# Key and query products of a delta-rule scan: plain stores, scatter in the loads, eight key rows first

## The reference, cut to what matters

```python
q = silu(causal_conv4(x @ Wq.T)); k = silu(causal_conv4(x @ Wk.T)) * SCALE; v = silu(causal_conv4(x @ Wv.T))
a = sigmoid(x @ Wa.T + ba); beta = sigmoid(x @ Wb.T + bb)
def step(S, inp):                       # S: batch, head, 64 value rows, 64 key columns
    qt, kt, vt, at, bt = inp
    err = einsum('bhij,bhj->bhi', S, kt) - vt
    S = at[..., None] * S - bt[..., None, None] * (err[..., None] * kt[:, :, None, :])
    return S, einsum('bhij,bhj->bhi', S, qt)
```

## Time and profile before

| | |
|---|---|
| runs | 7149.1, 7164.11, 7169.97 us; median 7164.11 |
| profiled execution, first to last instruction (span) | 7152.7 us |
| of it, the recurrence | to about 4300 us, 64 slots of about 65 us |
| busy over the span | DVE 76%, PE 70%, POOL 51%, PE weight loads 46%, ACT 46% |
| mean granted TensorE clock | 0.799 of full |

### The profile page before, as it was taken

How to read it: one execution, slowest core, us unless ns; L and a number is a source line. 1 busy time by engine, 2 the same in 40 slices (tenths; PEclk the granted TensorE clock), 3 DMA queues, 4 the chain that set the end, 5 groups by cost and what they waited for, 6 DMA issues and landing times. The chain is left out here.

```text
span 7152.7 us, 175742 instructions
## 1 busy us (share of the span) xinstructions
PE 5027.7 (70%) x58695; PEld 3318.4 (46%) x58695; DVE 5415.6 (76%) x15973; ACT 3322.6 (46%) x7234; POOL 3637.4 (51%) x4232
## 2 busy tenths in 40 slices
PE   5666666666666766666666644888878878888878
PEld 3555555555455555555555533333444443434443
DVE  5888889888888988888888864666666666666665
ACT  4554455444445444544454422444444444444444
POOL 3778778777777877787778771111111111111110
PEclk8777778777777777877777767888888888888888
DMA  4667666766766676667667742111111111111111
GB/s 124 156 158 163 165 152 160 167 160 148 166 162 161 158 166 163 155 158 170 153 157 164 170 107 64 43 50 51 45 45 44 44 48 44 44 44 44 44 45 37
DMA packets 1186126, 804.64 MB, mean 112 GB/s; under 512 B 1038563, under 2 KB 1090435, under 8 KB 1177220
## 3 DMA queue, kind: packets, MB, share of 16 engines
q1 hardware_dynamic: 878212, 610.17, 35.3%
q10 hardware_dynamic: 307200, 185.09, 10.6%
HBM read 490.57 MB, written 304.55 MB: 111 GB/s over the span
## 5 line engine op out<-in xcount | busy, mean ns | idle before, releaser
L464 POOL TENSOR_TENSOR qp<-qp,ab 128x512 f32<-128x512 f32 (+7 forms) x1024 | 937.3, 915 | 75.3
L469 POOL TENSOR_TENSOR qp<-qp,pt 128x512 f32<-128x512 f32 (+7 forms) x1024 | 912.8, 891 | 82.2 <-issue 2.0
L1771 DVE TENSOR_REDUCE nmax<-w_bank 128x1 f32<-128x512 f32 x1024 | 642.8, 684 | 408.0 <-PE w_bank L1353 403.1
L844 DVE SCALAR_TENSOR_TENSOR p_bank<-y,conv_w,p_bank 128x128 f32<-128x128 f32 x3072 | 828.1, 349 | 74.6 <-issue 25.0
L466 POOL TENSOR_TENSOR pt<-qp,vb 128x512 f32<-128x512 f32 (+7 forms) x1024 | 813.3, 794 | 9.2 <-DVE vb L921 9.2
L1308 POOL TENSOR_TENSOR ot<-ot,ln_w 128x1024 f32<-128x1024 f32 x64 | 151.1, 2361 | 1139.9 <-ACT ot L1610 1139.9
L530 PE MATMUL d_bank<-st 64*32 64x80 f32 x16384 | 490.1, 290 | 338.4 <-issue 319.1
L1313 POOL TENSOR_TENSOR x1b<-x,bias 128x256 f32<-128x256 f32 x64 | 46.4, 725 | 1162.7 <-DVE bst L1867 1162.7
L594 PEld LDWEIGHTS p_bank<-xnT,wqkv 128*128 128x128 f32 x4096 | 547.2, 215 | 192.2 <-issue 192.2
L502 PE MATMUL d_bank<-xd,kt 32*64 32x128 f32 x7936 | 342.4, 320 | 409.8 <-DVE st L862 393.2
L594 PE MATMUL p_bank<-xnT,wqkv 128*128 128x128 f32 x4096 | 596.5, 306 | 43.0 <-ACT st L676 31.3
(11 more groups left out here) (219 smaller groups left out, 11769.4 us busy)
## 6 DMA issues: line engine op xcount, KB each, us to landing
db<-decay_dram SPq DMA_DIRECT2D x124, 1024.0 KB, 12.3
prod_dram<-prod ACTq DMA_DIRECT2D x64, 1280.0 KB, 9.7
kp<-prod_dram SPq DMA_DIRECT2D x64, 640.0 KB, 4.4
qp<-prod_dram SPq DMA_DIRECT2D x64, 640.0 KB, 6.5
a_dram<-at ACTq DMA_DIRECT2D x64, 512.0 KB
ab<-a_dram SPq DMA_DIRECT2D x64, 512.0 KB, 5.9
v_dram<-vt ACTq DMA_DIRECT2D x64, 512.0 KB
vb<-v_dram SPq DMA_DIRECT2D x64, 512.0 KB, 7.1
```

Of the source, the lines that this page charges most:

```text
L464: link(nc.gpsimd.tensor_tensor(q, q, ab[:, g, r:r + 1, :].to_broadcast([128, w, DV]), ALU.mult), 1)
L469: link(nc.gpsimd.tensor_tensor(q, q, pt2[:, 0:w], ALU.add))
L844: nc.vector.scalar_tensor_tensor(out=zz, in0=y[:, j % Y_BANKS, i, :, tap:tap + C], scalar=conv_w[:, m, tap:tap + 1], in1=zz, op0=ALU.mult, ...
L1771: nc.vector.tensor_reduce(nmax[:, n:n + 1], bank[:], AX.X, ALU.max, negate=True).then_inc(freed, 1)
```

## The change

`prod_dram` gets the layout that the products have in SBUF: [128 rows, 32 blocks, 80]. ACT stores it in two DMAs, four batches each, the first as soon as the fourth batch is copied; every partition writes one contiguous run of 5,120 bytes in each. The waits for the earlier loads from the same DRAM tensor stand ahead of the copies, not behind them. The loads now gather pieces of 320 bytes: for each head h of four, one DMA into partitions h, h+4, h+8, ... . `kp` is loaded in two sets of four DMAs, rows 0 to 7 (semaphore `kp_in`) and rows 8 to 15 (`kl_in`), and `qp` in one set of four. In SP's order the first set, with its wait for both parts of the store, stands ahead of the `upd_dram` store; the rest stays behind it. DVE's first half waits for the first set alone, POOL for the second one and for `qp`.

```diff
-    prod_dram = [dram(f"prod_dram{g}", [GB * 4, P, ROW]) for g in range(GROUPS)]
+    prod_dram = [dram(f"prod_dram{g}", [P, GB * 4, ROW]) for g in range(GROUPS)]
...
+                if valid(lo + 1, hi + 1):
+                    rows = prod_dram[o].rearrange("(h k r) m c -> h k m r c", h=4, k=2)
+                    sp.wait_ge(*dma_of(p_wr, n, g, 1, 32))
+                    held(sp, sp_passed)
+                    if valid(lo, hi):
+                        sp.wait_ge(solve_chain, SOLVE_OPS * s + FIRST_HALF_OPS)
+                        held(sp, sp_passed)
+                    for h in range(4):
+                        sp.dma_start(kp[h:128:4, 0:HALF], rows[h, 0, :, 0:HALF]).then_inc(kp_in[o], 16)
                 if updates(lo, hi):
                     sp.wait_ge(solve_chain, SOLVE_OPS * (s + 1))
...
                     sp.dma_start(upd_dram[g].rearrange("b h t i -> (b h) (t i)"), eb[:]).then_inc(upd_wr[g], 16)
                 if valid(lo + 1, hi + 1):
-                    src = prod_dram[o].rearrange("m (h k r) c -> (m h) k r c", h=4, k=2)
-                    sp.wait_ge(*dma_of(p_wr, n, g, 1))
-                    held(sp, sp_passed)
-                    if due(SOLVE_OPS * s):
+                    if valid(lo, hi):
                         sp.wait_ge(solve_chain, SOLVE_OPS * s + solved(HALF))
                         held(sp, sp_passed)
-                    elif valid(lo, hi):
-                        sp.wait_ge(solve_chain, solved(HALF))
-                        held(sp, sp_passed)
-                    sp.dma_start(kp[:], src[:, 0]).then_inc(kp_in[o], 16)
-                if valid(lo + 1, hi + 1):
+                    for h in range(4):
+                        sp.dma_start(kp[h:128:4, HALF:C], rows[h, 0, :, HALF:C]).then_inc(kl_in[o], 16)
                     if due(dma_of(o_wr, n, g, -1)[1]):
                         sp.wait_ge(*dma_of(o_wr, n, g, -1))
                         held(sp, sp_passed)
-                    sp.dma_start(qp[:, o], src[:, 1]).then_inc(qp_in[o], 16)
+                    for h in range(4):
+                        sp.dma_start(qp[h:128:4, o], rows[h, 1]).then_inc(qp_in[o], 16)
...
-                pool.wait_ge(*dma_of(kp_in, n, g, 0))
+                pool.wait_ge(*dma_of(kl_in, n, g, 0, 64))
...
-                pool.wait_ge(*dma_of(qp_in, n, g, 0))
+                pool.wait_ge(*dma_of(qp_in, n, g, 0, 64))
...
             def products(s, n, g):
                 if due(dma_of(x_wr, n, g, -1, 32)[1]):
-                    act.wait_ge(*dma_of(p_wr, n, g, -1))
+                    act.wait_ge(*dma_of(p_wr, n, g, -1, 32))
                     act.wait_ge(*dma_of(x_wr, n, g, -1, 32))
-                for b in range(GB):
-                    act.wait_ge(p_filled, 8 * s + b + 1)
-                    nc.scalar.activation(prod[:, b, :], d_bank[b % 2][:, 0:4 * ROW], ACT.Copy).then_inc(p_freed, 1)
-                act.wait_ge(p_freed, 8 * s + 8)
                 if due(dma_of(qp_in, n, g, -2)[1]):
-                    act.wait_ge(*dma_of(qp_in, n, g, -2))
-                if due(dma_of(kp_in, n, g, -2)[1]):
-                    act.wait_ge(*dma_of(kp_in, n, g, -2))
-                act.dma_start(prod_dram[g].rearrange("m p c -> p m c"), prod[:].rearrange("p b (q c) -> p (b q) c", c=ROW)).then_inc(p_wr[g], 16)
+                    act.wait_ge(*dma_of(kp_in, n, g, -2, 64))
+                    act.wait_ge(*dma_of(kl_in, n, g, -2, 64))
+                    act.wait_ge(*dma_of(qp_in, n, g, -2, 64))
+                for first in (0, GB // 2):
+                    for b in range(first, first + GB // 2):
+                        act.wait_ge(p_filled, 8 * s + b + 1)
+                        nc.scalar.activation(prod[:, b, :], d_bank[b % 2][:, 0:4 * ROW], ACT.Copy).then_inc(p_freed, 1)
+                    act.wait_ge(p_freed, 8 * s + first + GB // 2)
+                    act.dma_start(prod_dram[g][:, 4 * first:4 * first + 2 * GB].rearrange("p m c -> p (m c)"),
+                                  prod[:, first:first + GB // 2].rearrange("p b c -> p (b c)")).then_inc(p_wr[g], 16)
...
-                    dve.wait_ge(*dma_of(kp_in, n, g, 0))
+                    dve.wait_ge(*dma_of(kp_in, n, g, 0, 64))
```

## The result

The changed kernel takes 7090.91 us (median of 4 runs, 7082.73 to 7096.39) against 7156.6 (4 runs, 7135.93 to 7169.97): ratio 0.9898, 95% interval 0.9878 to 0.9918. That is just past the end of the likeliest case's own range (7095, all of the wait back), and inside the wide one (7085 to 7190). The span fell from 7152.7 to 7080.9 us, 71.8 less. The last L942 begins at 4284.3 before and its counterpart L949 at 4204.8 after, so the recurrence gave 79.5 and the untouched rest varied by 7.7 the other way.

What follows compares the result with a forecast made beforehand. Bound: the recurrence's ring through DVE, the error exchange and PE, DVE also waiting for `kp`. Removed 67.3 us, given back 10 and 5, net 52: span 7100.7, plus 11.4 to the median, 7112 us; range 7085 to 7190.

Steps and rivals of the forecast that it cites:

- likeliest case: Recurrence: DVE's wait for `kp` goes, net 52 us, 7112 us; own range 7095 to 7137; chance 0.57.
- The cap: DVE's wait for `kp` at L911, 67.3 us in 25 slots: the most an earlier `kp` can give back.
- third rival: The product store is no faster, landing at 2012.3 as before: 7179 us, 7200 if instruction fetches are held up; chance 0.07.
- More than the cap: Rival: PE's stalls move with the traffic, 7080 us; chance 0.03.
- The store: Product store in the late slot lands at 2006.8 instead of 2012.3; bounds 2003.9 and 2009.2.
- The first eight rows: Four 82 KB key loads land at 2010.8, DVE wants them at 2012.7: wait gone, 1.9 us to spare.
- Gathers at the rate of `xd`: Rival: `kp` and `qp` gather slowly, 8.0 us more in SP's queue, 7231 us; chance 0.14.
- SP's order: Twelve loads of 0.52 us, 6.2 us, replace two taking 0.8; `e_dram` goes out some 0.9 us late, mostly covered.
- first rival: SP becomes the bound: late by a mean 0.8 us, 49 us more go, 7161 us; chance 0.19.
- Given back: Off the gain: 10 us for `e_dram` beyond its cover in 25 late slots, 5 us for late store landings.
- ACT: Second DMA issue, 0.39 us, between copies of batches 3 and 4, hidden by a 0.48 us wait for PE: nothing.
- The store is no faster: Rival: product store lands at 2012.3 as before, `upd_dram` waits behind it; 7179 us at least; chance 0.07.

Runs made afterwards that it cites:

- e9: Kernel before with its product store split in two DMAs, both issued after the eighth copy, old layout and order: 7154.87 us, ratio 1.0019.
- e6: Kernel before with the order alone: key rows 0 to 7 loaded ahead of `upd_dram`, old layout, single store: 7105.91 us, ratio 0.9934.
- e8: e2 with one wait more: SP issues the two `db` loads only when `xk` has landed: 7073.27 us, ratio 0.9893.
- e4: Kernel before with its store into the old layout split in two parts, the first issued after the fourth copy: 7089.17 us, ratio 0.9905.
- e11: Kernel before with two-part store and first eight key rows ahead of `upd_dram`, old layout (edits of e4 and e6): 7083.08 us, ratio 0.9917.
- e3: Changed kernel with one 1.31 MB store after the eight copies instead of two parts: 7116.73 us, ratio 0.9939.
- e10: Changed kernel with one store after the eighth copy and all gathers behind `upd_dram` (edits of e3 and e1): 7103.69 us, ratio 0.9941.
- e7: Changed kernel with each of the four query loads cut in two, four more DMA issues on SP: 7174.90 us, ratio 1.0030.
- e1: Changed kernel with the first set of four key loads, and its wait for the store, moved behind the `upd_dram` store: 7068.06 us, ratio 0.9880.
- e2: As e1, with `kp` loaded in one set of four DMAs of 16 rows, eight gathers a slot instead of twelve: 7069.10 us, ratio 0.9880.
- e12: e2 with the store in parts of six and two batches, the first issued after the sixth copy: 7083.30 us, ratio 0.9912.

## Why the prediction was right or wrong, point by point

- *The cap.* "The most that an earlier `kp` can give back" was put at 67.3 us. This step failed: a second term stood at nothing in the sum. 64.0 us of `kp` went, as forecast, and 24.7 of DVE's "issue" stalls in its first convolutions with them, 88.7 in all. The third rival spoke of instruction fetches that are held up, but only as a cost of a late store; that they were a cost already, and would be given back, is what the prediction missed.
- *What the stalls are.* The packets of the instruction queue q14 show it. In the kernel before, 24 of DVE's first convolutions stall, and in each of these slots one q14 packet of 8,192 bytes starts 3.2 to 5.4 us after the solve's end; the stalled instruction starts 1.73 to 1.99 us behind it. In three slots that packet starts by 3.0 us, and they have no stall; in the other 28 there is no such packet and no stall. In the changed kernel the first such packet comes at 1.5 us (median; 3.8 before). Over all runs 147 stalls follow such a packet by 1.7 to 2.2 us. By all of this DVE waits for an instruction fetch. The longest stall, and the queues from 1668 to 1673.5 us, while the product store (q10) kept the engines busy:

```profile
1675.45 1.65 DVE L844 SCALAR_TENSOR_TENSOR p_bank<-y,conv_w,p_bank 128x128 f32<-128x128 f32 x6 [2.52 <-issue]
```

```profile
q10 hardware_dynamic: 3194, 1.02, 94.7%
q1 hardware_dynamic: 1229, 0.42, 32.0%
q14 instruction: 1, 0.01, 0.5%
```

- *What makes the fetch late.* The stalls follow roughly how late the store is done: with `kp` out on the mean at 5.65 us (before), 5.53 (e9), 4.76 (e6), 4.51 (e8) they are 25.0, 18.0, 21.1 and 26.6 us; at 3.54 (e4), 3.09 (e11), 2.61 (e3), 2.51 (e10), 2.02 (e7) they are 9.1, 3.5, 9.1, 12.7 and 4.1; below 1.7 (e1, changed, e2, e12) 1.1 at most. e10 and e11 are out of order, so the store is not all of it, and that the fetch queues behind the store's packets is argued; no run isolated it.
- *More than the cap.* The case given 0.03 had the right side and named PE's stalls, not DVE's. PE's "issue" stalls ahead of L538 (now L543) did fall, from 147.7 to 85.8 us, but e4 gains 0.95% and still has 137.3.
- *The store.* Forecast at 3.6 us after the solve's end in the late slot, with bounds 0.7 and 6.0. After, the first load goes out 1.39 us after it on the mean, 3.6 at the most, and the second part lands 5.0 us after issue (median; 3.7 to 8.6). The reason for taking the middle, that the first part cannot run ahead of `v_dram`, was wrong: e4 moves half a megabyte there. One store alone would have been nearer to the forecast: 2.51 (e10).
- *The first eight rows.* In time in every slot but the first, as forecast, and sooner: 2.5 us to land. But this part of the change is not needed beside the other two (e1).
- *Gathers at the rate of `xd`.* Refuted: a spread gather of 82 KB lands in 2.5 us, the median `xd` load of 64 KB in 2.9. By the Trainium skill ("SBUF — State Buffer", Door 1: The DMA port swizzle) such gathers reach all ports, and this trace agrees so far as 82 KB into 32 spread partitions land in 2.5 us and 64 KB into 16 neighbours in 2.9 in the same kernel; no run set a gather into 16 neighbours against a spread one of the same bytes. The rival's own sum was also short: 8.0 us more on SP's queue would put the prediction's two slots 8.8 and 5.2 us behind DVE, not 5 and 3.
- *SP's order.* The cover ahead of `e_dram` was forecast to fall from 5.8 to about 2 us a slot: 1.8 measured, with a wait left in 54 of 61 slots. Two errors met: the store landed earlier, and a gather costs SP 0.61 us (median) and not 0.52, 0.76 in the slot shown. The price of a late SP, named as the first rival, is shown by e7.
- *Given back.* 15 us were taken off for `e_dram` and landings. The ledger has +35.7 for PE's update, which waits for `xd` (60.1 us against 16.6), and -27.4 at `xk`, whose load takes 7.5 us from issue in both kernels while DVE comes to it later: 8 net. The count by stage has 0.29 us a slot more, 18 in 61. So the size was about right, the path was not: the step named the later `xd`, but not who waits for it.
- *ACT.* The second issue cost nothing that can be seen: e4 has it and gains. The cover was misread: the 0.48 us of the earlier trace rows stand ahead of the fourth copy, and the fifth follows it at once; the cover is further on, where ACT waits 7.12 us for PE ahead of the seventh.
- *The store is no faster.* This rival did not come; e6 shows as well that `upd_dram` behind a late store does not turn the sign.

The other signs came as said: `xk` lands 26.4 us after the `e_dram` store goes out (26.3 before), and POOL's wait for it is 1.6 us a slot shorter.

What stays open: how much of the order's gain is the earlier and how much the smaller load, and what holds the fetch that DVE waits for.

## What to carry to other kernels

When several edits aim at one wait, the wait is paid once: here each of three alone took it away, or nearly, for 0.6 to 1% each, and all three together gave 1.0 to 1.1%. A transfer is cheapest where it starts before the DMA engines are full, so cut a store where its first half is ready and they have room; and a plain store paid for by many small loads moves the cost to the issuing queue, whose spare time must be counted first. Read the small rows of the waits too: time that nothing in the profile releases can go with the wait that is aimed at.

## What the runs showed of the hardware that was not expected

- A gather of 256 pieces of 320 bytes into 32 spread partitions takes SP 0.61 us to issue (median; `xd` with 256 pieces of 256 bytes 0.45, a plain `kp` load of 128 long runs 0.33).
- DMAs behind another one on ACT's queue move before that one has landed: 1.01 MB against 0.52 in the same stretch.
- Holding back 2.1 MB of `db` (e8) made `xk` only 0.9 us faster, though beside no `db` load, in the last two steps of the kernel before, it took 4.0 and 4.2.
- DVE's unexplained stalls each end 1.7 to 2.2 us after an 8,192-byte packet of the instruction queue q14 starts, in all 147 cases. The first such packet came 1.5 us (median) after a solve's end in the changed kernel and 3.8 in the one before.
